# A linear-attention and top-2 expert kernel: the experts' sums in steps of one unit, the denominators' epsilon on another engine, set-up copies ahead of memsets, and a new order of the steps on all engines

## The reference

```python
def block(x):                                   # x: (8 images, 128 channels, 48*48 tokens), float32
    x = x + linear_attention(layernorm_over_channels(x))
    t = tokens(x)                               # (8, 2304, 128)
    t = t + experts(layernorm(t))
    return channels(t)

def linear_attention(x):                        # 8 heads of 16; q, k = elu(.) + 1
    den = 1.0 / (sum_d(Q * cumsum(K, axis=1)) + 1e-10)      # axis 1 is the head axis
    num = causal sum over tokens of (q . k) v
    return num * den

def experts(x):                                 # 8 experts of 128 x 128, the 2 most probable are used
    logits = x @ gate + router_gamma
    combine = the 2 largest of softmax(logits), zero elsewhere
    return sum_e combine[e] * (gam[e] * (x @ W[e] + b[e]) + bet[e])
```

## Time and profile before

| | |
|---|---|
| median of 3 runs | 684.3 us (683.94 to 686.49) |
| the profiled execution, its own time | 687.47 us |
| its span, first to last instruction | 685.7 us |
| TensorE busy | 623.9 us, 91% of the span |
| VectorE busy | 626.5 us, 91% |
| GpSimd busy | 501.6 us, 73% |
| ScalarE busy | 437.5 us, 64% |
| DMA | 30.58 MB, mean 45 GB/s |
| mean granted clock of TensorE | 0.989 of full speed |

### The profile page before, as it was taken

One profiled execution on the slowest core, in us unless ns is written; L12 is line 12 of the kernel. 1 busy time (PEld: TensorE's weight loads), 2 busy tenths in 40 slices (PEclk: granted clock), 3 DMA queues, 4 the chain that ended last, 5 costly groups with the idle time before them and its releaser, 6 DMA issues.

```text
span 685.7 us, 37586 instructions
## 1 busy us (share of the span) xinstructions
PE 623.9 (91%) x13936; PEld 506.3 (74%) x14044; DVE 626.5 (91%) x2175; ACT 437.5 (64%) x1549; POOL 501.6 (73%) x745
## 2 busy tenths in 40 slices
PE   4769989999999999999999999999999999998875
PEld 3657777777777777777777777777777777777663
DVE  6778989999999999999999999999999999999774
ACT  1337656666667777666666667776776666667643
POOL 4747767777778888887778877878787787766631
PEclk9989999999999999999999999999999999999997
DMA  5211110111111111111111111111111121111001
GB/s 131 78 34 34 34 48 8 47 49 50 47 46 46 46 46 46 46 46 46 46 46 46 46 46 46 46 46 46 46 46 46 46 62 31 32 34 34 19 19 31
DMA packets 60234, 30.58 MB, mean 45 GB/s; under 512 B 2160, under 2 KB 60176, under 8 KB 60176
## 3 DMA queue, kind: packets, MB, share of 16 engines
q1 hardware_dynamic: 60176, 29.79, 15.5%
HBM read 20.34 MB, written 9.44 MB: 43 GB/s over the span
## 4 chain that ended last, share of the span: by engine, by line
PE 52%; DVE 24%; issue 15%; POOL 5%; DVEq 1%; ACT 1%; POOLq 0%; ACTq 0%
DVE total L824 4%; PE wide_b L1005 4%; PE num L1116 4%; PE wide_a L1212 4%; PE num L1081 3%; PE num L1099 3%; PE wide_a L1213 3%; PE wide_a L1214 3%; DVE bn L649 3%; DVE probs L696 3%; PE wide_a L1062 3%; DVE o L834 2%; PE bank_g L1037 2%; PE bank_g L975 2%; PE bank_g L1022 2%
## 5 line engine op out<-in xcount | busy, mean ns | idle before, releaser
L497 ACT ACTIVATE part<-wide_a,scale 128x128 f32<-128x128 f32 x576 | 156.3, 382 | 2.5 <-PE wide_a L1214 1.0
L373 POOL TENSOR_TENSOR two_sums<-part 128x512 f32<-128x512 f32 x72 | 92.9, 1290 | 32.0 <-ACT part L497 30.4
L1212 PE MATMUL wide_a<-e_high,x_high 128*128 128x512 f32 x216 | 97.8, 453 | 3.1 <-issue 1.1
L460 ACT ACTIVATE q_eo<-bank_g,parity 128x512 f32<-128x512 f32 x72 | 49.7, 690 | 67.5 <-PE bank_g L1037 67.5
L1214 PE MATMUL wide_a<-e_high,x_low 128*128 128x512 f32 x216 | 85.6, 396 | 0.0
L1213 PE MATMUL wide_a<-e_low,x_high 128*128 128x512 f32 x216 | 85.4, 395 | 0.0
L317 POOL TENSOR_TENSOR k_sum<-k_sum,feat 128x64 f32<-128x64 f32 x216 | 72.6, 336 | 16.9
L359 POOL TENSOR_TENSOR pack<-weight,pack 128x64 fp32r<-128x64 f32 x36 | 22.2, 616 | 77.1 <-ACT pack L505 77.1
L824 DVE SCALAR_TENSOR_TENSOR total<-wide_b,scale,total 128x128 f32<-128x128 f32 x216 | 58.8, 342 | 0.0
L824 DVE SCALAR_TENSOR_TENSOR total<-wide_a,scale,total 128x128 f32<-128x128 f32 x216 | 58.8, 342 | 0.0
L1212 PEld LDWEIGHTS wide_a<-e_high,x_high 128*128 128x128 f32 x216 | 41.6, 193 | 21.1 <-issue 17.2
(11 more groups left out here) (175 smaller groups left out, 2003.6 us busy)
## 6 DMA issues: line engine op xcount, KB each, us to landing
x<-in_x SPq DMA_DIRECT2D x36, 256.0 KB, 3.0
x_res<-in_x SPq DMA_DIRECT2D x36, 256.0 KB, 3.6
out<-o SPq DMA_DIRECT2D x36, 256.0 KB, 3.1
e_raw<-in_L_ffn_expert_w SPq DMA_DIRECT2D x1, 512.0 KB
beta_raw<-in_L_ffn_beta_w SPq DMA_DIRECT2D x1, 512.0 KB
w_raw<-in_L_conv_Wkv SPq DMA_DIRECT2D x2, 64.0 KB, 2.4
b_qkv<-in_L_conv_bkv SPq DMA_DIRECT2D x1, 128.0 KB, 5.9
w_raw<-in_L_conv_Wq SPq DMA_DIRECT2D x1, 64.0 KB, 2.6
```

What stands on the lines that cost most here:

```text
L373: tt(two_sums[:, g.par, two], part[:, two, 0:2], part[:, two, 2:4], ALU.add).then_inc(S[f"two_sums{p}"], 1)
L460: nc.scalar.activation(q_eo[:, g.par, :, e], bank_g[:].rearrange("p (u t) -> p u t", t=T), copy, scale=parity[:, e:e + 1]).then_inc(S[done ...
L497: last = nc.scalar.activation(part[:, u, e], w_bank[B_BANK[u]][:, 128 * e:128 * e + 128], copy, scale=scale[:, g.par, u, 4 + e:5 + e])
L1212: mm(out, x1_high[:, g.par, u], e_high[:, four], start=True, stop=False)
```

## The change

Six things are done.

1. `add_parts` and `experts_1_to_4` work on one unit instead of two. Per unit, GpSimd makes one step of 128x256. VectorE still makes four steps, but as two sums: experts 0 and 1 onto the first of GpSimd's two sums, 2 and 3 onto the second. TensorE transposes both totals. Every unit has its semaphores, so those who waited for a pair of units now wait for one.
2. The epsilon of the denominators is added on ScalarE instead of VectorE.
3. In the set-up, `v_pad`, `state` and `coef_t` are cleared on GpSimd instead of VectorE, and the copy of the transposed weights stands ahead of the two copies to `place`.
4. All four compute engines' steps have a new order (below), with ages renamed where the step's beginning was moved.
5. SP's step keeps its order (load of x, store, load of the residual), with ages 0, 6 and 2 instead of 0, 9 and 4.
6. GpSimd's and ScalarE's wait before overwriting x's parts is for projection 0 instead of 1, the last in the new order, and so is the deviation's wait for its evacuation.

The diff, cut to its core (waits renamed from pairs to units on TensorE are left out, as are the old orders):

```diff
             for e in range(EXPERTS):
                 made(nc.gpsimd.memset(order[:, :, e:e + 1], float(EXPERTS - e)))
+            made(nc.gpsimd.memset(state[:], 0.0))
+            for b in range(PAR):
+                made(nc.gpsimd.memset(v_pad[:, b], 0.0))
+                made(nc.gpsimd.memset(coef_t[:, b].bitcast(F32), 0.0))
...
-            def add_parts(g, p):
-                need(pool, f"part{2 * p}", g.i + 1)
-                need(pool, f"part{2 * p + 1}", g.i + 1)
+            def add_parts(g, u):
+                need(pool, f"part{u}", g.i + 1)
                 need(pool, "out_done", g.i - 1)
-                two = slice(2 * p, 2 * p + 2)
-                tt(two_sums[:, g.par, two], part[:, two, 0:2], part[:, two, 2:4], ALU.add).then_inc(S[f"two_sums{p}"], 1)
+                tt(two_sums[:, g.par, u], part[:, u, 0:2], part[:, u, 2:4], ALU.add).then_inc(S[f"two_sums{u}"], 1)
...
+            def denominators_eps(g):
+                need(act, "rden_done", g.i)
+                need(act, "den_sum", g.i + 1)
+                nc.scalar.activation(den1[:], den[:], copy, bias=1e-10).then_inc(S["den_eps"], 1)
...
-                for b in range(PAR):
-                    nc.vector.memset(v_pad[:, b], 0.0).then_inc(done, 1)
-                nc.vector.memset(state[:], 0.0).then_inc(done, 1)
                 nc.vector.memset(ins_window[:], 0.0).then_inc(done, 1)
-                for b in range(PAR):
-                    nc.vector.memset(coef_t[:, b].bitcast(F32), 0.0).then_inc(done, 1)
+                dve.wait_ge(S["first_pe"], 1)
+                copy(w_t[:], w_bank[0][:, 0:384]).then_inc(done, 1)
                 for n in range(2):
                     copy(place[:, n].rearrange("e (k j) -> e k j", j=2 * EXPERTS)[:, :, EXPERTS * n:EXPERTS * n + EXPERTS],
                          ident[0:EXPERTS, 0:EXPERTS].unsqueeze(1).broadcast_to([EXPERTS, EXPERTS, EXPERTS])).then_inc(done, 1)
-                dve.wait_ge(S["first_pe"], 1)
-                copy(w_t[:], w_bank[0][:, 0:384]).then_inc(done, 1)
...
-            def experts_1_to_4(g, p):
+            def experts_1_to_4(g, u):
                 need(dve, "out_done", g.i - 1)
-                need(dve, f"two_sums{p}", g.i + 1)
+                need(dve, f"two_sums{u}", g.i + 1)
                 need(dve, "scale_done", g.i + 1)
-                need(dve, f"a_{2 * p}", g.i + 1)
-                need(dve, f"a_{2 * p + 1}", g.i + 1)
...
+                need(dve, f"a_{u}", g.i + 1)
+                done, y = S[f"a_steps{u}"], w_bank[A_BANK[u]]
+
+                def add(e, before):
+                    return stt(total[:, g.par, u, e // 2], y[:, 128 * e:128 * e + 128], scale[:, g.par, u, e:e + 1], before,
+                               ALU.mult, ALU.add)
+
+                add(0, two_sums[:, g.par, u, 0]).then_inc(done, 1)
+                add(2, two_sums[:, g.par, u, 1]).then_inc(done, 1)
+                dve.wait_ge(done, 2 * g.i + 1)
+                add(1, total[:, g.par, u, 0])
+                dve.wait_ge(done, 2 * g.i + 2)
+                add(3, total[:, g.par, u, 1]).then_inc(S[f"a_sum{u}"], 1)
```

More of the change, by code:

```diff
@@ L254, in step @@
                     load_later(g)
-                g = at(9)
+                g = at(6)
                 if g:
                     store(g)
-                g = at(4)
+                g = at(2)
                 if g:
                     load_residual(g)
-            steps(sp, step, 9)
+            steps(sp, step, 6)
             for b in range(PAR):
@@ L836, in step @@
             def step(at):
+                g = at(5)
+                if g:
+                    second_rank(g)
                 g = at(4)
                 if g:
-                    denominators_eps(g)
+                    causal(g, 1)
+                    if first(g):
+                        bias_rows()
+                g = at(5)
+                if g:
+                    second_largest(g)
+                    both(g)
+                    picked_exp(g)
+                    coefficients(g)
+                    scales(g)
+                g = at(2)
+                if g:
+                    features(g, 1)
+                    features(g, 0)
+                    if first(g):
+                        gammas_and_gate()
+                g = at(0)
+                if g:
+                    statistics(g)
+                g = at(6)
+                if g:
+                    residual(g)
+                g = at(0)
+                if g:
+                    variances(g)
+                g = at(4)
+                if g:
+                    attention(g)
+                    if first(g):
+                        expert_weights()
+                g = at(3)
+                if g:
+                    denominators(g)
+                g = at(5)
+                if g:
+                    experts_1_to_4(g, 0)
+                    experts_1_to_4(g, 1)
+                g = at(3)
+                if g:
                     inverse_denominators(g)
@@ L1218, in output @@
                     pe.wait_ge(S["rest_dve"], REST_DVE)
-                need(pe, "a_sum0", g.i + 1)
-                need(pe, "a_sum1", g.i + 1)
+                for u in range(U):
+                    need(pe, f"a_sum{u}", g.i + 1)
                 need(pe, "squares_done", g.i + 2)
@@ L1227, in output @@
                 for u in range(U):
-                    out = bank_o[:, T * u:T * u + T]
-                    mm(out, two_sums[:, g.par, u, 1], ident[:], start=False, stop=False, is_transpose=True,
-                       skip_group_check=True)
-                    last = mm(out, total[:, g.par, u], ident[:], start=False, stop=(u == U - 1), is_transpose=True,
-                              skip_group_check=True)
+                    for k in range(2):
+                        last = mm(bank_o[:, T * u:T * u + T], total[:, g.par, u, k], ident[:], start=False,
+                                  stop=(u == U - 1 and k == 1), is_transpose=True, skip_group_check=True)
                 last.then_inc(S["out_done"], 1)
@@ L1237, in step @@
                 if g:
+                    experts(g, 0, 0)
+                    coef_transposed(g)
+                    experts(g, 3, 1)
+                    experts(g, 1, 0)
+                    experts(g, 2, 1)
+                g = at(5)
+                if g:
+                    x1_centred(g)
+                g = at(6)
+                if g:
+                    experts(g, 3, 0)
                     experts(g, 2, 0)
```

286 lines of the change are left out of this document (111 added, 175 removed).

## The result

The changed kernel takes 755.1 us (median of 4 runs, 754.76 to 756.02) beside 684.7 us for the kernel before: a ratio of 1.103, 95% interval 1.100 to 1.105. The forecast was 673 us, in a range from 664 to 684.

A forecast was written before the change was run, and what follows sets the result against it. VectorE's own queue was taken to set the 17.46 us period. Steady groups -6 (-0.2 x 30), set-up -2.8 and end -2.5 sum to -11.3 us, from the median 684.3 to 673.0; range 664 to 684.

The forecast's parts named there:

- VectorE's loop, 17.15 us: VectorE's queue per group in steady state: 17.46 us less 0.21 for epsilon and 0.10 for a wait filled by variances.
- the third rival: Steady state: one wait (second feature step, dearer hand-overs or late epsilon) eats VectorE's gain; period 17.45 to 17.6, 679 to 683 us; chance 0.20.
- Sums by unit: Experts' sums: VectorE keeps 16 steps per group, no gain or loss; GpSimd's four adds at 0.74 us, 0.4 more per group.
- The finer release: First projection needs one unit's four steps instead of eight, so TensorE may begin about 1 us earlier against VectorE.
- Features side by side, 0.1 us: VectorE's two consecutive feature steps: the second may wait for GpSimd's low part of the coefficients, 0 to 0.33 us per group.
- The loop through both engines, 17.2 us: TensorE's first expert product through projections, then VectorE's evacuations, router chain and mask back to it: 17.2 us per group.
- Set-up, -2.8 us: Before the first projection: clearing on GpSimd lets VectorE copy the weights 2.9 us earlier; -2.8 us, ends -3.3 and 0.
- the bound of 0: Set-up's worst end: no gain, if GpSimd's clearing, about as long as VectorE's, delays x's low part.
- SP's queue, 0: SP's loads and store with new ages: the next x lands before ScalarE needs it, cost 0.
- The end, -2.5 us: Last two groups: less adding and summing behind the last scaling, 2.5 us saved, ends -1 and -3.5.
- The slower rival: At the features: two GpSimd steps overtake VectorE's waiting second feature step, +39 us in the groups, 718 us; chance 0.13.

The follow-up runs named there:

- the kernel of 687.2 us: Changed kernel with TensorE's loop entered two groups earlier and clearing moved from GpSimd to VectorE, behind the copy of the weights and the first variances: 687.2 us, 1.0035.

## Why the prediction was wrong

**What it left out.** This is the step that failed: every step of the working takes it that TensorE has its instructions, so their supply stood at nothing, without a reason. No term and no rival had the start of the loop in it. The loop moved by 62 instructions, because the new order leaves 24 matmuls, their 24 weight loads and 14 waits out of the prologue, and that cost 64.4 us of the 70.4. The page before gave half of the warning: 39 packets on q8, the whole program once, so a loop of 103 KB that is held while it runs. No row says how near it was to not being held.

**VectorE's loop, 17.15 us (epsilon -0.21, variances -0.10).** It failed. VectorE was full, but right behind it came a chain through ScalarE's last scaling and GpSimd's add; with the epsilon alone VectorE won 0.33 us per group and lost 0.53 there. In the changed kernel with its loop moved the period is 17.48, which is the third rival's 17.45 to 17.6, but not by one of its waits: the second feature step is 0.12 us longer and not 0.33, the epsilon is late by 2.3 us in 28 groups.

**Sums by unit, "no gain and no loss".** Mis-sized: alone 8.7 us, of which (17.46 - 17.31) x 30 = 4.5 are period. And with it epsilon and variances gain, where without it they lose. GpSimd's four adds cost what I took: 0.733 us each in the changed kernel against 0.74. The finer release was named, and given no term.

**Features side by side, 0.1 us.** The length was right (0.12): VectorE keeps its turn, and GpSimd's product, 1.26 us at best, takes 1.72. In the old order the pair cost 15.5 us all the same, since only the step itself was priced, and not what stands behind it: the statistics, and the bank that they free. In the changed kernel no cost of the pair was found.

**The loop through both engines, 17.2 us.** The wait for the mask ahead of the first expert product came where it was foreseen (9.2 us over 28 groups in the kernel of 687.2). The turn of the loop, 0.27 us in every pass where the changed kernel has its branch, was not in the sum; moving the branch gave 7.1 us.

**Set-up, -2.8 us.** The first projection came 0.14 us later: the bound of 0, for a clearing that delays x's low part, looked at GpSimd's queue, and not at VectorE's steps beside it. With the clearing elsewhere the term was right: first projection at 11.4 us against a forecast of 11.3.

**The fill.** It had no term but the set-up. The first query-key product of GpSimd comes at 32.7 us against 25.2, and the first `o` at 86.5 against 79.4. Of the 7.5 us, 5.6 come from VectorE's statistics, which now stand behind the one-time weight copies, and these wait for TensorE; GpSimd's deviation, queued ahead of the keys, needs them. The statistics before and after:

```profile
19.47 0.88 DVE L649 BATCH_NORM_STATS2 bn<-bank_g 128x6 f32<-128x128 f32 x4
```

```profile
25.40 0.88 DVE L654 BATCH_NORM_STATS2 bn<-bank_g 128x6 f32<-128x128 f32 x4
```

**SP's queue, 0.** It held: no engine waits for a load from 60 to 690 us in the lists of the changed kernel and of that with its loop moved.

**The end, -2.5 us.** From the start of the last scaling to the end 9.41 us became 7.75: -1.7, within its ends.

**The slower rival** had the wrong place: GpSimd does overtake a VectorE step that already waits, but in the set-up, where it costs 2 to 3 us, and not at the features, where it would have cost 39. That the changed kernel is slower, as this rival had it, is luck: its mechanism did not come.

## What to carry to other kernels

Where an engine runs a long loop, look at the packets of its instruction queue: they should stop while the loop runs. Whatever changes the prologue moves the loop, and a move of 62 instructions cost 64 us here, where the change could win 22; compare a changed order only at a place that is not fetched again. When the fullest engine loses a step, ask which chain ends second: it needs its own gain, here single units, before the first gain shows.

## What the runs showed of the hardware

- A loop of 103.5 KB of TensorE instructions is run without being fetched again when it starts at instruction 3089, 3348, 5104 or 5112 of its program, and is fetched again at 5042 (every second pass) and at 5298 (every pass). Counted in packets of 256 instructions, the four lie between 16 ahead of a packet's start and 20 behind it, the two others 78 ahead of one. So counted, the loops at 5104, 5112, 5042 and 5298 all touch eight packets, so the number of packets touched does not tell the good from the bad. The Trainium skill, "Runtime: NRT & Kernel Launch", section "Instruction fetch mechanics", has blocks of 16 KiB, a store of 128 KiB for TensorE, and a stall at a taken branch whose target lies outside the current two blocks: the trace agrees on the block (1.52 MB in 93 packets) and on the stall (5.04 us), but not on the two blocks, since the loop's start lies 6.3 packets behind in all six programs, and four are not fetched again. It gives the branch as a reason to unroll in full; here that cost 20 us, added waits included. Why the two bad places differ, and where the border lies, stays open: no other place was tried.
- GpSimd's run of memsets shut VectorE's plain 128x128 step out for 3.56 us against 0.61: the waiting step did not get its turn between two memsets, and with the clearing on VectorE it took 0.61 us again. The Trainium skill, "SBUF — State Buffer", section "Who interferes with whom", has the lock for the length of one instruction; the trace shows a run of them.
- A written-out stream of TensorE instructions is not free: idle times of up to 1.3 us put down to issue, and 20 us in all, the added waits included.
